# A Gram product moved half a block earlier in TensorE's order (feed-forward stage, four-layer kernel, one core)

## The reference

```
h  = _ln(x) * g2 + beta2
ff = _gelu2(h @ W1 + b1) @ W2 + b2
return x + ff
```

```
for i in range(r):                      # r = 32
    q = Q[:, i]
    q = q / (jnp.linalg.norm(q) + EPS)
    Q = Q.at[:, i].set(q)
    coeffs = q @ Q[:, i + 1:]
    Q = Q.at[:, i + 1:].add(-jnp.outer(q, coeffs))
```

## Time and profile before

| | us |
|---|---|
| median of three runs | 3121.77 |
| the profiled execution | 3121.77 |
| its span | 3120.0 |
| feed-forward stage, PE at work in it | about 1385 to 2147 |
| PE busy over the span | 2788.0 (89%) |
| DVE busy over the span | 1901.0 (61%) |

### The profile page before, as it was taken

One profiled execution on the slowest core, in us unless ns is written; L12 is line 12 of the kernel. 1 busy time (PEld: TensorE's weight loads), 2 busy tenths in 40 slices (PEclk: granted clock), 3 DMA queues, 4 the chain that ended last, 5 costly groups with the idle time before them and its releaser, 6 DMA issues. The chain is left out here.

```text
span 3120.0 us, 45880 instructions
## 1 busy us (share of the span) xinstructions
PE 2788.0 (89%) x14065; PEld 2255.0 (72%) x14065; DVE 1901.0 (61%) x3706; ACT 1121.8 (36%) x2255; POOL 1030.7 (33%) x752
## 2 busy tenths in 40 slices
PE   6964999999999999969999999996998988988986
PEld 3424788888888888857888888885776766766774
DVE  8954878777787778765444443443565555555443
ACT  1114778777776877731111111111111111111111
POOL 1005667565666767443100111002322222122100
PEclk9987999999999999989999999998999999999997
DMA  4225776767667676632000000001533332333310
GB/s 163 95 89 150 208 200 181 208 179 203 190 196 195 184 206 186 186 114 75 27 28 28 28 9 20 28 14 56 165 112 98 100 100 93 102 96 98 98 31 34
DMA packets 255618, 356.47 MB, mean 114 GB/s; under 512 B 26570, under 2 KB 113610, under 8 KB 252682
## 3 DMA queue, kind: packets, MB, share of 16 engines
q1 hardware_dynamic: 253610, 350.20, 37.7%
q0 software_dynamic: 1760, 3.19, 0.4%
HBM read 268.91 MB, written 34.05 MB: 97 GB/s over the span
## 5 line engine op out<-in xcount | busy, mean ns | idle before, releaser
L819 POOL TENSOR_TENSOR at_bias<-at_bias,at_mask 128x1024 f32<-128x1024 f32 x224 | 480.8, 2149 | 366.6 <-DMA at_bias<-in_fside_Bx16xSxS 365.0
L1218 DVE TENSOR_TENSOR at_pL<-at_bank_probT,at_pH 128x512 fp32r<-128x512 f32 x512 | 351.5, 686 | 207.4 <-ACT at_pH L930 205.2
L923 ACT ACTIVATE at_y<-at_bias,at_nmax 128x512 f32<-128x512 f32 x512 | 368.4, 719 | 57.9 <-DVE at_nmax L1212 56.6
L930 ACT ACTIVATE at_pH<-at_bank_probT 128x512 fp32r<-128x512 f32 x512 | 304.6, 595 | 204.8 <-PE at_bank_probT L1073 199.5
L1212 DVE CUSTOM_DVE_ANT_0 at_bias<-at_bias,at_bank_score 128x512 f32<-128x512 f32 x512 | 346.6, 677 | 4.5 <-PE at_bank_score L1065 2.2
L1589 POOL TENSOR_SCALAR expert_WH<-expert_stage 128x1024 fp32r<-128x1024 f32 x128 | 153.2, 1196 | 584.9 <-PE expert_bank_out L98 459.9
L1073 PE MATMUL at_bank_probT<-at_ident,at_y 128*128 128x128 f32 x2048 | 310.8, 274 | 35.2 <-DVE at_pL L1218 29.1
L1662 ACT ACTIVATE expert_g<-expert_bank_hid,expert_b1c 128x512 f32<-128x512 f32 x128 | 88.3, 690 | 648.4 <-PE expert_bank_hid L98 648.4
L1073 PEld LDWEIGHTS at_bank_probT<-at_ident,at_y 128*128 128x128 f32 x2048 | 246.1, 141 | 95.8 <-ACT at_y L923 27.9
L1662 ACT ACTIVATE ff_g<-ff_bank_hid,ff_b1c 128x512 f32<-128x512 f32 x128 | 88.3, 689 | 611.6 <-PE ff_bank_hid L98 611.6
L1906 DVE CAST ff_gH<-ff_g 128x512 fp32r<-128x512 f32 x128 | 69.8, 546 | 390.5 <-ACT ff_g L1662 390.4
(11 more groups left out here) (311 smaller groups left out, 6325.0 us busy)
## 6 DMA issues: line engine op xcount, KB each, us to landing
at_bias<-in_fside_Bx16xSxS SPq DMA_DIRECT2D x256, 512.0 KB, 4.7
expert_stage<-in_L_cond_Wi SPq DMA_DIRECT2D x128, 256.0 KB, 2.7
expert_stage<-in_L_cond_Wo SPq DMA_DIRECT2D x128, 256.0 KB, 2.8
at_q<-at_nat SPq DMA_DIRECT2D x384, 64.0 KB, 3.5
at_k<-at_nat SPq DMA_DIRECT2D x384, 64.0 KB, 2.9
st_f<-in_x SPq DMA_DIRECT2D x8, 1024.0 KB, 7.4
x_after_layer<-st_y SPq DMA_DIRECT2D x8, 1024.0 KB, 4.8
at_x<-x_after_layer SPq DMA_DIRECT2D x32, 256.0 KB, 4.0
```

What stands on the lines that cost most here:

```text
L819: pool.tensor_tensor(bias[i % NB][:, :, :], bias[i % NB][:, :, :], mask[:, 2 * i % R:2 * i % R + 2, :], ALU.add).then_inc(s_bm, 1)
L923: act.activation(prob[u % 2][:, :], bias[u // 2 % NB][:, u % 2, :], ACT.Exp, scale=-1.0, bias=nmax[:, u % 4:u % 4 + 1], accum_out=sums[:, ...
L930: act.activation(pH[u // 2 % 2][:, :, u % 2, :], pT[u % 2][:, :].rearrange("p (k q) -> p k q", q=P), ACT.Copy).then_inc(s_pth, 1)
L1218: dve.tensor_tensor(pL[u // 2 % 2][:, :, u % 2, :], pT[u % 2][:, :].rearrange("p (k q) -> p k q", q=P), f32(pH[u // 2 % 2][:, :, u % 2, :] ...
```

## The change

Two edits, both in PE's program. Within `gram_schmidt` the four L1768 matmuls belong to blocks with f % 4 == 0 rather than f % 4 == 1. Within a block `gram_schmidt` is called last, behind `output(n, f - 1)`, rather than between `hidden(n, f)` and `output`.

```
             def gram_schmidt(n, f):
-                if f % 4 == 1:
+                if f % 4 == 0:
                     i = n * GS + f // 4
                     pe.wait_ge(s_prod, i + 1)
-                    if f == 1:
+                    if f == 0:
                         pe.wait_ge(s_h32, (n + 1) * C)
...
                 for f in range(FC):
                     hidden(n, f)
-                    if not expert:
-                        gram_schmidt(n, f)
                     if f > 0:
                         output(n, f - 1)
                     if expert and not first:
                         tail(n - 1, 1 - slot, f)
+                    if not expert:
+                        gram_schmidt(n, f)
```

## The result

The changed kernel takes 3156.64 us, the median of six runs (3152.3 to 3160.5), against 3124.47 us for the kernel before in the same runs (3118.88 to 3128.99): +32.2 us. The ratio is 1.0103, 95% interval 1.0092 to 1.0113. The forecast was 3152.5 us, +30.7 us, range 3141 to 3160.

A forecast was written before the change was run, and what follows sets the result against it. PE was taken to bound the feed-forward stage. Waits at the first column 20.7, refills 0.9, other columns 1.5 and clock 7.6 sum to 30.7 us; 3121.8 + 30.7 = 3152.5 us, range 3141 to 3160.

The forecast's parts named there:

- PE sets the pace: Feed-forward stage: PE's order sets the time, so time PE loses is added to the end.
- Part 1: First column of each sample (f = 0): PE waits for `prod` behind `hidden(n, 0)`, eight waits, 20.7 us.
- sample 0 would pass its delay on: Sample 0: block 0's delay shifts the whole chain, the 2.59 us weight-part wait stays, no credit taken.
- The refills: After each f = 0 wait the second matmul comes 0.34 after the first instead of 0.23: 0.9 us.
- Part 2: Columns f = 4, 8, 12: `output` covers nearly all; 1.5 us, with sample 0 waiting 0.52 (f = 12) and 0.18 (f = 8).
- the 0.6 us: f = 12 of samples 1 to 6: `prod` 0.15 late for the weight load, taken as 0.1 x 6.
- Part 3: Matmuls after the f = 0 waits: the clock falls to 1.2 GHz, 6 x 1.26 = 7.6 us.
- Six of eight: Clock after the f = 0 waits: falls after 6 of 8, rather more often than two of three in the rows.
- The clock stays up: Rival: PE waits at f = 0 but the dense stream keeps 2.4 GHz; +23.1 us, 3144.9 us, chance 0.20.
- Every wait breaks the stream: Rival: queue runs dry at all 24 places of f = 4, 8, 12; 9.8 instead of 1.5, 3160.8 us, chance 0.12.
- The product is there in time: Rival: `prod` runs in DVE's 1.53 us idle gap ahead of the high part; 8 x 0.1, 3122.6 us, chance 0.03.
- The rule on short idles: Skill rule on PE idles between matmul groups: all eight f = 0 waits would cost, 10.1 rather than 7.6 us.

The follow-up runs named there:

- the filled one: The changed kernel with 11 more 128 x 512 matmuls, result unused, ahead of each sample's first Gram product; ratio 1.0085 to the kernel before, +22.5 us.

## Why the prediction was right

- *PE sets the pace.* Held. 21.4 us more outside matmuls and 13.2 us more in them make 34.6 us of stage; DVE's, ACT's and POOL's busy times did not move.
- *Part 1, the first column.* The sum was 20.7 us. In sample 3 the start came 2.94 us after the last matmul of `hidden` where 0.23 is free, 2.71 against the 2.63 worked out; in samples 1 to 6 the Gram matmuls start 0.13 after `prod` ends, where the prediction took 0.05 from the earlier trace rows. Read in this way the eight add up to 21.2 us. The list has 19.9 for them, as it does not count the stretch in which the last matmul is still drawn as running. That nothing would cover the wait, and that sample 0 would pass its delay on, also held: the 2.6 us wait for the weight part stayed.
- *The refills.* The 0.9 us for them were not there. In the kernel before, too, the second matmul behind the Gram matmuls comes 0.32 after the first, so this was paid already, and in samples 1 and 4, where the clock held, the Gram matmuls and the next twelve take what they took before.
- *Part 2, the others.* The matmuls of blocks 4, 8 and 12 of samples 1 to 7 have no wait, so the 0.6 us were not there. Zero is also what the prediction had read, beside its sum, from the Trainium skill's rule on weight loads taken ahead (TensorE: Matmul & The Clock Gate, section Architectural detail), but it did not come about in that way: the ones were not in place early, their load waited for `prod` at block 12 and could be late without cost. In sample 0, block 12, the wait is 1.83 us as listed (2.0 from start to start) and not 0.52, and the 0.18 at block 8 was not there, so Part 2 measured 2.0 against 1.5. The reason is on the timeline: in the kernel before `hidden(0, 12)` ran at the low clock, in this one at the full clock, so PE came to the same `prod` earlier. The low clock came behind the new wait instead. One was traded for the other. Other profiles agree: where the low clock did not follow the weight part's wait (the kernel with all but the first column moved) the wait at block 12 is 1.82 us, where it did (the filled one) 0.38.
- *Part 3, the clock.* This is the term that was mis-sized, 7.6 us for what measured 11.3. That it falls after six of the eight is what was taken, and what was seen; the price of a fall was too low. I had 1.26 us, from a block in which the low clock was on already when the wait ended. In sample 3 it begins within `hidden(3, 1)`: eight starts from 1698.46 to 1701.83 take 3.37 us instead of 1.82, so 1.55. The Gram matmuls and the next twelve together took 1.6 to 1.7 us longer than before in samples 0, 2, 3, 5 and 6, 0.02 in samples 1 and 4, and 3.15 in sample 7, where the low clock lasted twice as long: 11.3 in all.
- *The parts together.* 21.2 + 2.0 + 11.3 = 34.5 us, against the stage's 34.6. The kernel with only the first column moved gives the same account: 21.1 of waits and 9.8 of six falls, none double, are 30.9 against its 30.8.
- *Six of eight was partly luck.* The share was raised from two of three, but those three rows were picked from more. The attention stage of the same trace has 14 waits of PE of 1.67 to 2.78 us, and the low clock follows three; windows behind three of the 14 are shown below this list. The reason given for raising the share was not tested.
- *Why the total fits better than its parts.* The stage was forecast at +30.7 and came at +34.6. The profiled pair differs by only 31.4 over the span, because the stages ahead took 2.5 us less in the later execution. The medians of the runs give +32.2. The agreement to 1.5 us is therefore partly luck; the agreement of the mechanism is not.
- *The rivals.* "The clock stays up" would have been +23.1: that is nearly what the kernel with the filled wait shows (stage +21.8), so its price was right and its condition did not hold. "Every wait breaks the stream" fell with the experiment that moves only those columns (+2.2 in the stage). "The product is there in time" needed another order on DVE. Given that order, the cost is nearly gone, as the rival's condition had it. But the 1.53 us of idle time ahead of the high part were those of sample 3; in sample 2 of the same trace DVE has only 0.64, and the residual fills the rest.
- *The rule on short idles.* The Trainium skill (same page, section A second HAM failure mode) says that idles of PE between groups can make the clock go back and forth. The runs bear it out further than the trace of before did: 2 of 8 waits of 1.0 to 1.4 us, 6 of 8 of 2.5 us, and 26 of 32 closely spaced ones were followed by the low clock; those of 0.5 and 0.8 us were not. That all eight would cost, as the prediction read it, did not happen.

Three windows of the kernel before, in its attention stage, behind waits of 1.76, 2.00 and 2.19 us:

```profile
610.00:615.00 5.00, 4.78 (x29) 4.07 (x30) 4.71 (x16) 3.19 (x8) 4.66 (x5) 1.00 0.72 186
817.50:820.70 3.20, 3.20 (x17) 3.02 (x15) 0.39 (x3) 0.87 (x2) 1.13 (x2) 0.50 0.77 213
957.50:960.60 3.10, 3.10 (x10) 2.32 (x9) 2.60 (x7) 1.94 (x5) 0.00 (x0) 0.50 0.74 197
```

## What to carry to other kernels

Before an instruction is moved forward in one engine's order, find its producer on the other engine and measure how long the producer's chain is from the last thing that your engine did, here 2.7 us more than PE's stream leaves between two matmuls. Then count what stands between. With 12 matmuls of 0.227 us between, the move was free; with none it cost the whole chain, once per sample. And on TensorE add the clock to a wait of one to three microseconds: here it added about half as much again. Price a fall from rows in which the whole low stretch falls on work, and count all the waits of that length in the trace, not the two or three nearest.

## What was not expected of the hardware

- The low clock behind waits of the same length comes and goes. In the changed kernel samples 1 and 4 were spared, in the one with only the first column moved samples 2 and 6, with the same waits of about 2.5 us. Counted over the eleven profiles of this document (the two kernels and nine experiments, one execution each): of waits of 1.1 us or less in the attention and feed-forward stages none was followed by it; of PE's waits for `prod` of 1.8 us and more, 41 of 51; of the 2.6 us wait for the weight part in sample 0, the same in every kernel, 5 of 11; of the waits of 1.6 to 2.9 us in the attention stage, 46 of 147. What decides it in the single case was not tried.
- The same falls move the whole program from one execution to the next. No experiment edited the attention stage, yet it has 1 to 8 low stretches, and the time spent in them goes with where the feed-forward stage begins: 1382.5 to 1386.4 in the five profiles with 3 to 14 us at the low clock there, 1388.3 to 1388.8 in the four with 17, 1392.8 and 1394.0 in the two with 31 and 27.
- With waits close together (32 of 2.4 us on average) the clock's penalty per us of wait is not clearly larger. It was 56 us for 76.9 us of waits, 0.73 per us; with eight of them it was 13.2 for 21.4, 0.62, in the changed kernel and 9.8 for 21.0, 0.47, with the first column alone.
- An instruction on DVE can start late with "issue" as its only reason, at the top of the loop: 0.73 and 0.54 us after the one ahead of it in samples 3 and 5 of the kernel with `prod` ahead of the split, and without any gap in samples 1, 2, 4, 6 and 7. Why was not tried.
